# Second graph layer: projection and neighbour sums merged into one stage that runs in place order, its row gathers begun after ten stored tiles; ScalarE zeroes layer 0's second accumulator

## The reference, cut to what matters

```python
def _sage_conv(x, src, tgt, W_l, b_l, W_r):
    n = x.shape[0]
    msgs = x[src]
    agg = jax.ops.segment_sum(msgs, tgt, num_segments=n)
    deg = jax.ops.segment_sum(jnp.ones((src.shape[0],), x.dtype), tgt, num_segments=n)
    agg = agg / jnp.maximum(deg, 1.0)[:, None]
    return agg @ W_l + b_l + x @ W_r
h = jax.nn.relu(_sage_conv(x, src, tgt, W_l1, b1, W_r1))
logits = _sage_conv(h, src, tgt, W_l2, b2, W_r2)
```

## Time and profile before

| what | us |
|---|---|
| median of 3 runs (2958.1 to 2959.84) | 2958.7 |
| profiled execution | 2963.02 |
| its span, first to last instruction | 2960.8 |
| layer 0: first gather to the projection's first DVE instruction | 1738.1 to 2129.4 |
| projection: to layer 1's first gather | 2129.4 to 2170.3 |
| layer 1: to the last stage's first DVE instruction | 2170.3 to 2755.6 |
| last stage | 2755.6 to 2960.8 |

### The profile page before, as it was taken

One profiled execution on the slowest core, in us unless ns is written; L12 is line 12 of the kernel. 1 busy time (PEld: TensorE's weight loads), 2 busy tenths in 40 slices (PEclk: granted clock), 3 DMA queues, 4 the chain that ended last, 5 costly groups with the idle time before them and its releaser, 6 DMA issues. The chain is left out here.

```text
span 2960.8 us, 35471 instructions
## 1 busy us (share of the span) xinstructions
PE 2468.8 (83%) x8644; PEld 1444.2 (49%) x8644; DVE 1909.6 (64%) x3873; ACT 1019.1 (34%) x2851; POOL 1809.9 (61%) x1880
## 2 busy tenths in 40 slices
PE   5588997289999999989998858888777777778799
PEld 2144443045555555546666645555444444343577
DVE  8997876267777777744535656666654444444888
ACT  1277778157776777742222210000110000000232
POOL 5777777767676767630037757777547777777200
PEclk8799999589999999999999989999777777876899
DMA  9222324079999999982056665555343333333001
GB/s 281 72 84 85 96 88 160 14 218 269 263 264 266 262 263 265 266 245 74 27 167 204 201 191 168 169 169 166 94 133 106 105 105 106 106 105 105 22 1 45
DMA packets 238394, 446.46 MB, mean 151 GB/s; under 512 B 47451, under 2 KB 129005, under 8 KB 237999
## 3 DMA queue, kind: packets, MB, share of 16 engines
q0 software_dynamic: 96288, 254.83, 31.9%
q1 hardware_dynamic: 136416, 184.09, 19.0%
q10 hardware_dynamic: 5488, 5.28, 0.5%
HBM read 320.06 MB, written 126.13 MB: 151 GB/s over the span
## 5 line engine op out<-in xcount | busy, mean ns | idle before, releaser
L1780 POOL DMA_INDIRECT nbr_yg<-y_d,gidx x763 | 721.6, 946 | 245.4 <-PE nbr_sum L1890 130.7
L1890 PE MATMUL nbr_sum<-nbr_yg,nbr_hot 128*128 128x258 f32 x1526 | 603.9, 503 | 216.3 <-DMA nbr_yg<-y_d,gidx 169.9
L887 POOL DMA_INDIRECT qg<-q_d,rb x480 | 481.8, 1004 | 207.7 <-DVE hb L973 114.3
L1828 DVE TENSOR_TENSOR nbr<-nbr_sum,nbr 128x258 f32 x763 | 323.6, 424 | 435.6 <-PE nbr_sum L1890 411.4
L1890 PEld LDWEIGHTS nbr_sum<-nbr_yg,nbr_hot 128*128 128x128 f32 x1526 | 299.8, 232 | 503.6 <-DMA nbr_yg<-y_d,gidx 187.9
L413 POOL DMA_INDIRECT recs_d<-recs,slot_src x416 | 409.5, 984 | 150.3 <-issue 138.5
L1004 PE MATMUL p_sum<-hb,wide 128*96 128x512 f32 x960 | 452.1, 593 | 2.6 <-ACT hb L933 2.6
L933 ACT ACTIVATE hb<-hb 128x512 f32<-128x512 f32 x480 | 295.9, 630 | 208.8 <-DVE hb L973 207.3
L973 DVE TENSOR_TENSOR hb<-p_h,qg 128x512 f32<-128x512 f32 x480 | 310.1, 680 | 21.6 <-DMA qg<-q_d,rb 20.0
L1278 POOL DMA_INDIRECT n_ahead<-y_d,gidx x165 | 156.7, 949 | 268.2 <-DMA y_d<-n_y 200.6
L437 ACT ACTIVATE lane_hot<-bare_hot,val 128x128 f16<-128x128 f16 x832 | 247.5, 392 | 123.5 <-DVE bare_hot L671 123.5
(11 more groups left out here) (321 smaller groups left out, 3466.5 us busy)
## 6 DMA issues: line engine op xcount, KB each, us to landing
agg_d<-agg SPq DMA_DIRECT2D x240, 192.4 KB, 5.2
msg_d<-n_ahead SPq DMA_DIRECT2D x165, 128.0 KB, 2.7
nbr_ys<-msg_d SPq DMA_DIRECT2D x165, 128.0 KB, 2.5
nbr_yg<-y_d,gidx POOLq DMA_INDIRECT x763, 2.8
p_low<-p_d SPq DMA_DIRECT2D x11, 768.0 KB, 12.4
recs_d<-fill SPq DMA_DIRECT2D x16, 510.0 KB
rb<-recs_d SPq DMA_DIRECT2D x60, 136.0 KB, 4.9
qg<-q_d,rb POOLq DMA_INDIRECT x480
```

Source lines behind the costliest of these rows:

```text
L887: pool.indirect_dma_start(qg[t % QB][:, :], None, S.q[:, :], bass.IndirectOffsetOnAxis(ap=rb[n % RB][:, t % BT, 1:2].bitcast(U32), axis=0) ...
L1780: pool.indirect_dma_start(yg[n % YB][:, 0:D], None, S.y[:, :], bass.IndirectOffsetOnAxis(ap=C.gidx[:, FROM + n:FROM + n + 1], axis=0)).the ...
L1828: dve.tensor_tensor(nbr, p_sum[t % SUMS][:, 0:W], nbr, ALU.add).then_inc(s_acc, 1)
L1890: pe.matmul(p_sum[t % SUMS][:, 0:W], hot[t // BT % HOTS][:, column, :], rows[:, :], start=True, stop=True).then_inc(s_sum, 1)
```

## The change

- `stage_project` and layer 1 of `stage_neighbours` become one stage, `stage_second_neighbours`; `stage_neighbours` keeps layer 0 alone and is named `stage_first_neighbours`.
- The merged stage works in place order. DVE reads the five chunk numbers into registers at its start and takes `C.nbr` by register; the reciprocal degrees are copied into place order, five at a time (`rdeg_at`). The stores to `y_d` have fixed addresses. Layer 0 writes `C.z` by place, and layer 1 adds `C.x2` by place and writes `C.z` by tile.
- POOL issues the gathers of the 165 early tiles once the first ten stores to `y_d` have landed, and waits at tile 165 for all 25. There are 18 row buffers in place of 6. Three gathers in a row share a semaphore, and PE waits for all three before the first of them.
- The PSUM banks of the projection (three `turn`, three `out`) serve as the six banks of the sums.
- DVE builds the first three one-hot blocks between the projection's copies, behind tiles 11, 14 and 17.
- ACT clears `C.nbr` for layer 1, behind its last copy of the projection, from the float16 zeros `zeros_w`; in layer 0 ACT clears `of_stored` in the same way while DVE clears `C.nbr`.
- The semaphores of the projection are cleared by SP in the middle of the stage.

Layer 0, cut to the lines that differ in order:

```diff
             @block.scalar
             def _(act):
-                for tile in range(NT if layer == 0 else 0):
-                    if tile % CH == 0:
-                        own = load_own_buckets(nc, act, C.tile_at[:, tile:tile + CH], NT - 1)
-                    act.wait_ge(s_z, tile + 1)
-                    act.activation(C.z[:, bass.ds(own[tile % CH], 1), :].rearrange("p a d -> p (a d)"), p_z[:, 0:D],
-                                   ACT.Copy).then_inc(s_z_taken, 1)
+                act.activation(of_stored[:, :, :],
+                               C.zeros_w[:, 0:W].rearrange("p (a n) -> p a n", a=1).to_broadcast([P, NT, W]),
+                               ACT.Copy).then_inc(s_nbr_zero, 1)
+                for place in range(NT):
+                    act.wait_ge(s_z, place + 1)
+                    act.activation(C.z[:, place, :], p_z[:, 0:D], ACT.Copy).then_inc(s_z_taken, 1)
...
                 one_hot(0)
                 one_hot(1)
                 dve.memset(C.nbr[:, :, :], 0.0).then_inc(s_nbr_zero, 1)
-                if layer == 0:
-                    dve.memset(of_stored[:, :, :], 0.0).then_inc(s_nbr_zero, 1)
-                dve.wait_ge(s_nbr_zero, 3 - layer)
+                dve.wait_ge(s_nbr_zero, 2)
```

The merged stage, cut to its loops (`relu`, `transposes`, `one_hot`, `accumulate` and `product` are as before but for the place order):

```diff
+def stage_second_neighbours(nc, C, A, S):
...
+        HB, XB, YB, MEANS, RELUS = 6, 6, 6, 5, 4
+        BT, GB, PER, HOTS, SUMS, EVERY = 8, 18, 3, 3, 6, 16
+        HOT_AFTER = {11: 0, 14: 1, 17: 2}
...
+            @block.sync
+            def _(sp):
...
+                for p in range(NT):
+                    sp.wait_ge(out.empty, p + 1)
+                    sp.dma_start(S.y[p * P:(p + 1) * P, :], y[p % YB][:, :]).then_inc(s_yst[p % YB], 16)
...
+                sp.wait_ge(s_acc, NSTORED + 1)
+                for sem in of_projection:
+                    sp.sem_clear(sem)
+
+            @block.gpsimd
+            def _(pool):
+                for b in range(GB):
+                    pool.memset(yg[b][:, D:W], 1.0).then_inc(s_zero, 1)
+                for b in range(YB):
+                    pool.wait_ge(s_yst[b], 16 * len(range(b, EARLY_NODES // P, YB)))
+                for t in range(NTILE):
+                    if t == NSTORED:
+                        for b in range(YB):
+                            pool.wait_ge(s_yst[b], 16 * len(range(b, NT, YB)))
+                    if t >= GB:
+                        pool.wait_ge(s_sum, t - GB + 1)
+                        pool.nop(nofuse=True)
+                    pool.indirect_dma_start(yg[t % GB][:, 0:D], None, S.y[0:EARLY_NODES, :] if t < NSTORED else S.y[:, :],
+                                            bass.IndirectOffsetOnAxis(ap=C.gidx[:, t:t + 1], axis=0)
+                                            ).then_inc(s_gath[t // PER % len(s_gath)], 16)
+
+            @block.scalar
+            def _(act):
...
+                act.wait_ge(s_h, NT)
+                act.activation(C.nbr[:, :, :], C.zeros_w[:, 0:W].rearrange("p (a n) -> p a n", a=1).to_broadcast([P, NT, W]),
+                               ACT.Copy).then_inc(s_nbr_zero, 1)
+
+            @block.vector
+            def _(dve):
...
+                def mean(p):
+                    if p % CH == 0:
+                        dve.tensor_copy(rdeg_at[:, p // CH, :],
+                                        C.rdeg[:, :, :].rearrange("p (c a) b -> p c (a b)", a=CH)[:, bass.ds(chunks_at[p // CH], 1), :]
+                                        .rearrange("p a n -> p (a n)")).then_inc(s_deg_at, 1)
+                        dve.wait_ge(s_deg_at, p // CH + 1)
...
+                chunks_at = load_own_buckets(nc, dve, C.chunk_at[:, 0:NCH], NCH - 1)
...
+                for p in range(NT):
+                    product(p)
+                    if p + MEANS < NT:
+                        mean(p + MEANS)
+                    if p in HOT_AFTER:
+                        one_hot(HOT_AFTER[p])
+                dve.wait_ge(s_nbr_zero, 1)
+                for t in range(NTILE):
+                    if t % BT == 0:
+                        buckets = load_own_buckets(nc, dve, C.bucket[0:1, 1, t:t + BT], NT - 1)
+                    accumulate(t, buckets[t % BT])
...
+            @block.tensor
+            def _(pe):
...
+                pe.wait_ge(s_zero, GB)
+                for t in range(NTILE):
...
+                    if t == len(tr.banks):
+                        pe.wait_ge(out.empty, NT)
+                    if t >= SUMS and t % 2 == 0:
+                        pe.wait_ge(s_acc, t - SUMS + 2)
+                    if t % PER == 0:
+                        b = t // PER % len(s_gath)
+                        pe.wait_ge(s_gath[b], C.gathered[b] + 16 * (PER * (t // GB) + min(PER, NTILE - t)))
+                    pe.matmul(p_sum[t % SUMS][:, 0:W], hot[t // BT % HOTS][:, t % BT, :], yg[t % GB][:, :], start=True,
+                              stop=True).then_inc(s_sum, 1)
...
-            stage_neighbours(nc, C, A, S, 0)
-            stage_project(nc, C, A, S)
-            stage_neighbours(nc, C, A, S, 1)
+            stage_first_neighbours(nc, C, A, S)
+            stage_second_neighbours(nc, C, A, S)
```

More of the change, by code:

```diff
@@ L1602, in stage_nodes, with stage_first_neighbours @@
         m.clear_sems()
[L1605 removed]
+def stage_first_neighbours(nc, C, A, S):
     with ExitStack() as ctx:
[L1610 to L1695 removed]
@@ L1698, in stage_neighbours @@
-def stage_neighbours(nc, C, A, S, layer):
-    W_r = A.W_r1 if layer == 0 else A.W_r2
-    with ExitStack() as ctx:
-        m = Mem(nc, ctx, f"nbr{layer}_")
+        m = Mem(nc, ctx, "nbr0_")
         BT = 8
@@ L1709, in stage_neighbours @@
         assert EVERY * NT < NTILE
-        KB = 8 if layer == 0 else 0
+        KB = 8
         yg = [m.sb(f"yg{b}", [P, W]) for b in range(YB)]
@@ L1713, in stage_neighbours @@
         hot = [m.sb(f"hot{b}", [P, BT, P]) for b in range(HOTS)]
-        of_stored = m.sb("of_stored", [P, NT, W]) if layer == 0 else None
+        of_stored = m.sb("of_stored", [P, NT, W])
         w_r, b_r = m.sb("w_r", [P, KD, D]), m.sb("b_r", [1, D])
@@ L1720, in stage_neighbours @@
         s_w, s_z, s_z_taken, s_nbr_zero, s_last = (m.sem(n) for n in ("w", "z", "z_taken", "nbr_zero", "last"))
+        s_iota = m.sem("iota")
         s_gath, s_back = [m.sem(f"gath{b}") for b in range(YB)], [m.sem(f"back{b}") for b in range(KB)]
+        C.s_gath, C.gathered = s_gath, [16 * len(range(b, NTILE - NSTORED, YB)) for b in range(YB)]
         STORED_AT, DIRECT_AT = (1, 3, 6), (0, 2, 4, 5, 7)
-        FROM = NSTORED if layer == 0 else 0
-        mixed = MIXED if layer == 0 else 0
+        FROM, mixed = NSTORED, MIXED
         NEW = PERIOD - STORED_PER
@@ L1832, in join @@
                     dve.tensor_tensor(C.nbr[:, tile, :], C.nbr[:, tile, :], of_stored[:, tile, :], ALU.add).then_inc(s_joined, 1)
-                JOIN = PERIOD * MIXED if layer == 0 else NTILE
-                dve.tensor_copy(p_iota[:, 0, :], C.iota_f[:, :]).then_inc(s_nbr_zero, 1)
-                dve.wait_ge(s_nbr_zero, 1)
+                JOIN = PERIOD * MIXED
+                dve.tensor_copy(p_iota[:, 0, :], C.iota_f[:, :]).then_inc(s_iota, 1)
+                dve.wait_ge(s_iota, 1)
                 one_hot(0)
@@ L1848, in _ @@
                         join(t - JOIN, t)
-                    tile, at = divmod(t - 2, EVERY)
-                    if layer == 1 and at == EVERY - 1 and 0 <= tile < NT:
-                        dve.wait_ge(s_z, tile + 1)
-                        place = load_own_buckets(nc, dve, C.place_of[:, tile:tile + 1], NT - 1)[0]
-                        dve.tensor_tensor(C.z[:, tile, :], p_z[:, 0:D],
-                                          C.x2[:, bass.ds(place, 1), :].rearrange("p a d -> p (a d)"), ALU.add
-                                          ).then_inc(s_z_taken, 1)
                     n, at = divmod(t, BT)
@@ L1858, in _ @@
                         one_hot(n + 2)
-                if layer == 0:
-                    for tile in range(NTILE - JOIN, NT):
-                        join(tile, NTILE - 1)
+                for tile in range(NTILE - JOIN, NT):
+                    join(tile, NTILE - 1)
             @block.tensor
```

222 lines of the change are left out of this document (127 added, 95 removed).

## The result

| | before | after |
|---|---|---|
| median of 4 runs each, us | 2959.27 | 2936.81 |
| lowest to highest | 2958.1 to 2967.01 | 2935.06 to 2938.27 |
| profiled execution / its span | 2963.02 / 2960.8 | 2938.27 / 2936.5 |

The ratio is 0.9917, with a 95% interval of 0.9904 to 0.9931: 22.5 us faster. The prediction was 2932.2 us with a range of 2928 to 2941. Sign, size and range hold; the forecast was 4.6 us too fast.

What follows compares the result with a forecast made beforehand. GpSimd's gathers, 1.25 us each, were taken to bound layer 1. Terms -6.0 - 19.3 - 2.1 + 0.9 = -26.5 us took the median from 2958.7 to 2932.2 us, with 8 in 10 for 2928 to 2941.

Steps and rivals of the forecast that it cites:

- Layer 0: Start of layer 0: second clear moved to ScalarE, so VectorE's first addition and the eleventh gather come earlier, 6.0 us gained.
- First gather of layer 1: Border from projection to layer 1: first gather follows the tenth store instead, 19.3 us earlier.
- the register load and the small copy: Start of the merged stage: one load of registers taken at 0.8 us, one copy of 5 elements at 0.2.
- The stall at the eighth gather: Start of layer 1: the eighth gather, 2.07 us behind the 1.25 us pace, would no longer wait, 2.1 us gained.
- rival 1: Beside the projection: VectorE's work shuts GpSimd out; full 2946 us, chance 0.04, mild 2935 to 2938, chance 0.08.
- Its full form: No gather runs beside VectorE's work in the projection: layer 1 in effect 14 us later, 2946 us, chance 0.04.
- The gather of 1.55 us in the earlier trace: Gather at 1570.02 beside a wide two-input add, 0.6 us longer, cited for GpSimd being shut out by VectorE.
- the gather at 1568.76: Gather said to lie wholly beside VectorE's float32 tensor_scalar yet take 0.95 us, cited against GpSimd being shut out.
- the figures of 620 and 3100 ns: Skill page's figures: a DMA of 620 ns took about 3100 ns beside a float32 VectorE copy.
- The tail: End of layer 1: groups of three make one more tile wait for the last gather, 0.9 us added.
- Rival 2: Layer 0 does not pass its gain on, TensorE and VectorE having eight tiles in five gathers: 2938 us, chance 0.07.
- rival 3: Layer 1's pace was set by buffers, 18 of them shorten it to 0.95 us a gather: 2793 us, chance 0.01.
- rival 4: All of layer 1: groups of three make TensorE the bound, 1.43 us a tile, 81 us more, 3013, chance 0.04.

Runs made afterwards that it cites:

- e3: Changed kernel, but GpSimd waits for all 25 stores before its first gather of layer 1: 2960.95 us, ratio 0.9990 to the kernel before.
- e4: Changed kernel with 6 row buffers and a wait for every gather, still begun after ten stores: 2950.01 us, ratio 0.9948 to the kernel before.
- e5: Changed kernel with 12 row buffers and waits for pairs of gathers: 2945.52 us, ratio 0.9926 to the kernel before.
- e7: Changed kernel without layer 1's own product (150 matmul instructions left out on TensorE): 2944.03 us, ratio 0.9925 to the kernel before.
- e8: Changed kernel with 18 semaphores, TensorE waiting for each gather by itself: 2942.46 us, ratio 0.9918 to the kernel before.
- e2: Kernel before with one edit alone, ScalarE clears of_stored in layer 0: 2958.95 us, ratio 0.9981 to the kernel before.
- e12: Changed kernel run again, nothing altered: 2942.79 us, ratio 0.9913 to the kernel before.
- e11: Changed kernel with means eight tiles ahead, chunk registers loaded in layer 0 and a semaphore for each of 18 buffers: 2940.04 us, ratio 0.9905 to the kernel before.
- e1: Changed kernel, but VectorE clears both accumulators of layer 0 again: 2949.31 us, ratio 0.9948 to the kernel before.
- e6: Changed kernel, but VectorE clears C.nbr for layer 1 behind its last projection copy: 2938.94 us, ratio 0.9910 to the kernel before.
- e10: Changed kernel, but VectorE loads the five chunk numbers into registers in mid layer 0: 2938.99 us, ratio 0.9906 to the kernel before.
- e9: Changed kernel with nine h buffers and means eight tiles ahead instead of five: 2939.69 us, ratio 0.9901 to the kernel before.

## Why the prediction was right

It was right in its main step: layer 1 is 463 steps of 1.25 us behind its first gather, whatever the other engines do. So the sum had only to find when the first gather comes and whether one is ever late. e3, e4, e5, e7 and e8 each moved something else and left that step at 1.250 us. Point by point:

- **Layer 0, forecast -6.0, measured -6.8** (first gather included) in the two profiles, and -5.6 (2.7 to 8.3) for this edit alone in e2. The mechanism is as told. The first addition was forecast at 1749.10 and TensorE's tile 6 at 1750.63, and they stand at 1749.25 and 1750.61. The term was a little small behind that: I moved the eleventh gather by as much as that tile (6.0), but it moved 7.1, and 7.25 counted from the first gather. From tile 6 to this gather it was 3.72 us and is 2.63, because these tiles now run at the higher clock. Before, the clock had risen at 1749.9 and fell again at 1753.3, while TensorE stood still for 6 us; after, it rises at 1751.4 and stays. The window 1740 to 1760 has 0.59 before and 0.71 after.
- **First gather of layer 1, forecast -19.3 beyond layer 0, measured -17.2.** The term was over-sized by 2.1 us. For the register load and the small copy I had 1.0 together; the first copy out of PSUM came 1.7 later behind the last gather of layer 0 (1.23 at the border, 0.49 behind it): +0.7. The nine copies took 0.2 more. From the tenth copy to the gather I had 2.6 and it was 3.8: +1.2. Of this, 0.7 is the tenth store, which took 2.41 us and not 1.7, and 0.5 lies around it: 0.93 us from its landing to the gather where I had 0.3, less 0.2 at its issue. In every kernel that waits for ten stores the tenth is the last to land, as far as the traces have the landings; it took 1.7 us in five of them and up to 3.6 (e12), and so this stretch was between 3.05 and 4.96 us.
- **The stall at the eighth gather, forecast -2.1, measured -1.35.** The old stall is gone, and 0.7 us came back in three longer gathers beside the projection (the one of 1.20 us above, a second of 1.20 at 2150.33, one of 1.13 at 2158.09). That is rival 1 at its mildest: the earlier trace rows had a gather that took 0.6 us more, and here it is 0.2 to 0.25 us for three of the fourteen gathers that run beside the projection. Its full form (14 us) is ruled out. The traces also show which work of VectorE does it: not the copies out of PSUM nor the one-hot blocks, but the means, which read two operands from SBUF. The gather of 1.20 us at 2147.57 went 0.09 us after the mean at 2147.48, shown above. In the 14 traces 51 gathers of these two layers take over 1.00 us, and every one began 0.05 to 0.27 us after such an instruction (a mean, the joining of `of_stored` at the end of layer 0, in e7 the addition of `C.x2` to itself) and ended 0.81 to 0.83 us after its end. The gather of 1.55 us in the earlier trace rows fits: the add ends at 1570.74 and the gather 0.83 us later. It is not certain to happen, for 9 of 58 gathers that began like that were not stretched. Of the gather at 1568.76 I said too much: only its first half lies beside the tensor_scalar. The Trainium skill, page "SBUF — State Buffer", section "Who interferes with whom", names beside the two-port modes, which alone I took from it, another case: a VectorE instruction with two inputs in SBUF contends with a GpSimd instruction that reads SBUF. The traces agree with this one, by 0.7 us in all; the figures of 620 and 3100 ns stand in another section of that page, and no gather here was held up by nearly as much.
- **The tail, forecast +0.9, measured +0.6, and the border behind it, not in the sum, +1.7.** They belong together. In the kernel before, in e2, e4 and e5 the last stage follows the last addition by 0.75 us. In the other ten profiles the addition does not matter: the last stage begins 6.83 us behind the last gather in the eight kernels that have 18 buffers and groups of three, and 7.81 in e8 and e11, which have 18 semaphores, while the last addition moves between 3.87 and 4.89. So what the border waits for there hangs on GpSimd's last gather, and not on the sums, and it comes only with 18 buffers. What it is stays open, for the profile shows nothing on GpSimd in these microseconds.
- **The last stage, not in the sum, -1.3.** It takes 203.9 to 205.0 us in the merged kernels with the same code and 205.1 and 205.2 in the two others, so most of this is scatter, and it came in the forecast's favour.
- **From the profile to the median.** The stretches sum to -24.3 us by the spans, where the forecast had -26.5: 2.2 us of error. The medians differ by 22.5 only, since the profiled execution before stood 3.8 us above its median and that after 1.5: 1.8 us. And the median of the kernel before is 2959.27 with the fourth run and not 2958.7: 0.6 us. Together these are the 4.6 us. The 2.2 us are a balance: +2.1, +0.75 and +1.7 on one side, -0.8, -0.3 and -1.3 on the other. Without the second group they would have been 4.6, so part of the closeness is luck. The measured 2936.8 lies just outside the forecast's own bounds of 2929 to 2936, and inside the range that allowed for rivals 1 and 2.

Rival 2 is refuted by e1 and e2, rival 3 by e4 and e5, rival 4 by e7 and e8. Of the edits that I had put at nothing, the clear of layer 1 on ScalarE is at nothing by e6. The one-hot blocks in the projection were not undone in any run: its last 15 copies take 20.8 us with them and 19.4 before, so TensorE leaves it later, and with 18 buffers no gather waits for that. The place order was not undone either; what it is seen to cost is the load of registers and the small copies at the stage's start.

## What to carry to other kernels

When one engine issues without a gap through a long stage, price a change by two numbers only: when the first instruction of that chain can go, and how many of its steps will be late; a faster helper, a better clock or less work elsewhere is worth nothing (TensorE's busy time here was anything from 220 to 311 of 400 us, at one pace). Buffers beyond the pace's need pay exactly for a head start, and their number follows from how long the consumer is still busy elsewhere. If a chain starts on a landing, give its term the spread of landings (here 1.7 to 3.6 us for the same store) and not the median alone, and price each border between stages by itself, at a few us, from the last instruction of the engine that paces the stage and not only from the last result.

## What the runs showed of the hardware that was not expected

- **A gather that GpSimd begins just after a VectorE instruction with both operands in SBUF usually waits for it.** 51 gathers took up to 1.20 us instead of 0.945 in this way beside instructions of 0.43 to 0.48 us, and one 1.55 us beside an add of 1.49. None of the 51 stood beside only additions, copies or compares that read one operand from PSUM, although those keep VectorE busy 47% of layer 1.
- **TensorE's clock falls for up to 10 us in the middle of a stage in which it is over 80% busy.** Layer 0 of the changed kernel has 1.00 in the windows from 1760 to 2060; e1 has 0.97 and 0.95 in two of them and e11 0.97 and 0.94, with 3.9 and 5.7 us lost by gathers at places where it fell to between 0.55 and 0.83. e10 has e11's program in that layer and none of it, and e4, e5, e6 and e9 have shorter falls (3.4 us) in the changed kernel's program, with 1.3 us lost in e5. So it is scatter between executions: 375.2 and 382.3 us for the same code, which can turn one profile into a false verdict on an edit.
- **More work in bursts, higher clock.** At the same work and pace the granted clock in layer 1 was 0.82 to 0.86 with TensorE served in groups of three (seven kernels), 0.78 in pairs (e5) and 0.76 to 0.80 one by one (five kernels); with a sixth of its matmuls left out (e7) it was 0.80, not higher.
- **A load of five registers on VectorE costs 1.24 us** at the beginning of a stage (9.30 against 8.06 us behind the last gather, ten profiles against two). Without it the first instruction took 0.60 us and not 0.18, so that 0.83 us were left.
- **The store of 128 KB mostly lands after 1.7 us before the gathers begin, but single ones of the first ten took up to 3.7** (e8); over all 25 of the changed kernel the median is 1.9 and the longest 3.9.
